# A macaron layer on one core: four row blocks turned by SBUF transfers and VectorE instead of TensorE

## The reference

```python
x = x + 0.5 * ffn(layernorm(x))
x = x + attn(layernorm(x))
x = x + 0.5 * ffn(layernorm(x))

def ffn(x):
    x_prev = concat([zeros(B, 1, C), x[:, :-1, :]], axis=1)
    xr = mu_r * x + (1 - mu_r) * x_prev
    xk = mu_k * x + (1 - mu_k) * x_prev
    r = sigmoid(xr @ W_r.T)
    return r * (square(relu(xk @ W_k.T)) @ W_v.T)

def attn(x):                       # 16 heads of 16
    q, k = relu(x @ Wq.T) / 4, relu(x @ Wk.T) / 4
    v, u = x @ Wv.T, silu(x @ Wu.T)
    out = srms_norm(q @ (k.T @ v)) * u     # per head; k.T @ v over all tokens
    return out @ Wo.T
```

## Time and profile before

| | |
|---|---|
| median of 3 runs | 312.24 us |
| the profiled execution | 310.67 us |
| its span | 308.9 us |
| PE busy | 301.8 us, 98% |
| DVE busy | 240.9 us, 78% |
| ACT busy | 235.5 us, 76% |
| POOL busy | 215.1 us, 70% |
| granted TensorE clock | 1.0 of full speed throughout |

### The profile page before, as it was taken

One profiled execution on the slowest core, in us unless ns is written; L12 is line 12 of the kernel. 1 busy time (PEld: TensorE's weight loads), 2 busy tenths in 40 slices (PEclk: granted clock), 3 DMA queues, 4 the chain that ended last, 5 costly groups with the idle time before them and its releaser, 6 DMA issues.

```text
span 308.9 us, 5806 instructions
## 1 busy us (share of the span) xinstructions
PE 301.8 (98%) x2035; PEld 275.2 (89%) x2035; DVE 240.9 (78%) x585; ACT 235.5 (76%) x461; POOL 215.1 (70%) x237
## 2 busy tenths in 40 slices
PE   6999999999999999999999999999999999999995
PEld 4888889988988998998988998989999999999984
DVE  5899875666856946985994799596989797999695
ACT  3979669699589679679269358579797979699981
POOL 4598978789687686669278315726797979758823
PEclk9999999999999999999999999999999999999999
DMA  7960000000000000000000000000001011101123
GB/s 217 382 217 3 0 1 2 2 0 0 3 0 3 0 0 2 0 2 0 0 3 1 2 0 0 2 1 3 0 3 68 11 59 36 35 2 68 39 100 136
DMA packets 10752, 10.85 MB, mean 35 GB/s; under 512 B 482, under 2 KB 10724, under 8 KB 10724
## 3 DMA queue, kind: packets, MB, share of 16 engines
q1 hardware_dynamic: 10432, 10.23, 9.6%
q10 hardware_dynamic: 292, 0.26, 0.2%
HBM read 6.29 MB, written 4.19 MB: 34 GB/s over the span
## 4 chain that ended last, share of the span: by engine, by line
PE 74%; DVE 14%; ACT 4%; POOL 3%; issue 2%; DMA 1%; DVEq 0%; ACTq 0%
PE psK L1293 7%; PE psK L1295 7%; PE psK L1294 7%; PE psX L1293 7%; PE psX L1295 7%; PE psX L1294 7%; PE psRV L1293 6%; PE psRV L1294 6%; PE psRV L1295 6%; DVE mix L957 3%; PE psA L1310 3%; PE psA L1498 2%; PE psX L1511 2%; PE psX L1425 2%; PE psK L1498 2%
## 5 line engine op out<-in xcount | busy, mean ns | idle before, releaser
L957 DVE SCALAR_TENSOR_TENSOR mix<-psA,mu,mix 128x512 f32<-128x512 f32 x60 | 41.5, 745 | 10.0 <-ACT mix L642 10.0
L625 ACT ACTIVATE xn<-xs,shiftA,rstdA 128x256 f32<-128x256 f32 x53 | 27.7, 607 | 16.3 <-POOL shiftA L417 16.3
L433 POOL TENSOR_TENSOR mix_k_lo<-mix,mix_k_hi 128x512 fp32r<-128x512 f32 x26 | 33.2, 1299 | 8.2 <-ACT mix_k_hi L675 8.2
L642 ACT ACTIVATE mix<-psA,one_mu 128x511 f32<-128x511 f32 x60 | 36.9, 697 | 0.0
L1293 PE MATMUL psRV<-ffn_hi,mix_r_hi 128*128 128x256 f32 x120 | 34.3, 286 | 0.0
L1295 PE MATMUL psRV<-ffn_hi,mix_r_lo 128*128 128x256 f32 x120 | 33.6, 280 | 0.0
L1294 PE MATMUL psRV<-ffn_lo,mix_r_hi 128*128 128x256 f32 x120 | 33.5, 279 | 0.0
L1293 PE MATMUL psRV<-ffn_hi,act_hi 128*128 128x256 f32 x96 | 27.5, 287 | 0.2 <-POOL act_lo L455 0.2
L1294 PE MATMUL psRV<-ffn_lo,act_hi 128*128 128x256 f32 x96 | 26.8, 280 | 0.0
L1295 PE MATMUL psRV<-ffn_hi,act_lo 128*128 128x256 f32 x96 | 26.8, 279 | 0.0
L485 POOL TENSOR_TENSOR k_lo<-k_tok,k_hi 128x512 fp32r<-128x512 f32 x14 | 18.1, 1292 | 11.5 <-ACT k_hi L730 11.5
(11 more groups left out here) (210 smaller groups left out, 1081.3 us busy)
## 6 DMA issues: line engine op xcount, KB each, us to landing
xs<-x_dram SPq DMA_DIRECT2D x7, 512.0 KB, 7.8
out_dram<-xs SPq DMA_DIRECT2D x7, 512.0 KB, 2.9
out_dram<-xs SPq DMA_DIRECT2D x4, 128.0 KB, 1.8
xs<-x_dram ACTq DMA_DIRECT2D x2, 128.0 KB, 2.8
xs<-x_dram SPq DMA_DIRECT2D x2, 128.0 KB, 2.6
silu_u<-w_ffn_k_dram SPq DMA_DIRECT2D x1, 256.0 KB, 4.7
silu_u<-w_ffn_r_dram SPq DMA_DIRECT2D x1, 256.0 KB, 5.8
q_store<-w_k_dram SPq DMA_DIRECT2D x1, 256.0 KB, 6.0
```

The costliest lines, as they stand in the source:

```text
L433: nc.gpsimd.tensor_tensor(mix_k_lo[:, h, :], mix[:, 0, h, :], mix_k_hi[:, h, :].bitcast(F32), ALU.subtract).then_inc(s_lo_k, 1)
L625: nc.scalar.activation(xn[:, t, :], tile_row(xs, b, t), ACT.Identity, bias=shiftA[:, t:t + 1], scale=rstdA[:, t:t + 1]).then_inc(s_xn, 1)
L642: nc.scalar.activation(mix[:, rk, h, 1:BLOCK], psA[:, h, 0:BLOCK - 1], ACT.Copy, scale=one_mu[:, rk, h:h + 1]).then_inc(s_prev, 1)
L957: nc.vector.scalar_tensor_tensor(out=m, in0=psA[:, h, :], scalar=mu[:, rk, h:h + 1], in1=m, op0=ALU.mult, op1=ALU.add).then_inc(s_mix, 1)
```

## The change

For the blocks 3, 4, 5 and 6 (`TURNED`), the eight transposes of `transpose_a` on PE go. In their place SP issues 16 transfers inside SBUF for each block, each of a 32x32 grid element of the 4x4 grid of the 128x128 squares (32 partitions, 8 pieces of 32 float32 each): they move row group i and column group j to their place in `quads`, a view of the tile `squares`. Then `turn` on DVE transposes the 32x32 squares, two instructions of 128x512, from `quads` to `psA`. The normalized rows are written to `xn` and `gout` by turns. The rows are made an iteration ahead: those of block i+2 are made in iteration i, as before, but now from scales that POOL makes first in that iteration, and from statistics that DVE makes in the iteration before (from block 5 on); the turn on DVE comes an iteration later, where PE's transposes were. Block 3 is made within iteration 1 and turned in iteration 2.

```diff
+        TURNED = range(3, 7)
+        QUAD = 32
+        QUADS = P // QUAD
+        quads = squares[:].rearrange("p g e -> p (g e)")
+        def rows_of(n):
+            return gout if n in TURNED and n % 2 == 0 else xn
+        def turned_before(n):
+            return 2 * n - 2 * (n in TURNED and n > TURNED[0])
...
+            for n in TURNED:
+                sp.wait_ge(*normalized(n, TILES - 1))
+                if n > TURNED[0]:
+                    sp.wait_ge(s_tA, 2 * n)
+                for j in range(QUADS):
+                    for i in range(QUADS):
+                        rows = quads[j * QUAD:(j + 1) * QUAD, i * D:(i + 1) * D]
+                        sp.dma_start(rows.rearrange("c (th f) -> c th f", f=QUAD),
+                                     rows_of(n)[i * QUAD:(i + 1) * QUAD, :, :].rearrange(
+                                         "c t (h j f) -> c (t h) j f", h=HALVES, j=QUADS)[:, :, j, :]
+                                     ).then_inc(s_quads, 16)
...
             for i in range(1, 6):
+                if 2 <= i <= 4:
+                    scales_a(i + 2)
                 act_low(i)
+                if i == 1:
+                    scales_a(3)
                 k_low(i + 1)
                 if i > 1:
                     kt_low(i - 1)
-                scales_a(i + 2)
+                if i == 5:
+                    scales_a(7)
                 scales_b(i)
...
-                    act.wait_ge(s_tA, 2 * n)
+                    act.wait_ge(s_tA, turned_before(n))
...
-                    nc.scalar.activation(xn[:, t, :], tile_row(xs, b, t), ACT.Identity,
+                    nc.scalar.activation(rows_of(n)[:, t, :], tile_row(xs, b, t), ACT.Identity,
...
                 if i == 1:
                     x2_high(a)
-                activate_k(i)
-                if a is not None and i > 1:
+                    activate_k(i)
+                else:
+                    if i in (3, 4):
+                        normalize(i + 2, (0, 1))
+                    activate_k(i, (0,))
                     x2_high(a)
+                    activate_k(i, (1,))
+                    if i == 2:
+                        normalize(4)
+                    elif i < 5:
+                        normalize(i + 2, (2, 3))
                 if nxt is not None:
                     previous(nxt)
...
-                if i <= 5:
+                if i in (1, 5):
                     normalize(i + 2)
...
+            def turn(n, free=()):
+                for s, v in free:
+                    dve.wait_ge(s, v)
+                dve.wait_ge(s_halo, n + 1)
+                dve.wait_ge(s_quads, 16 * QUADS * QUADS * (n - TURNED[0] + 1))
+                blocks = quads.rearrange("p (i t h f) -> p h t i f", i=QUADS, t=TILES, h=HALVES)
+                for h in range(HALVES):
+                    nc.vector.transpose(psA[:, h, :].rearrange("p (t i c) -> p t i c", t=TILES, i=QUADS),
+                                        blocks[:, h, :, :, :]).then_inc(s_tA, 1)
...
-            def projections(a):
+            def projections(a, n=None):
                 for t in range(TILES):
+                    if n is not None:
+                        bn_rows(n, (t,))
                     silu(a, t)
 
             for i in range(1, 7):
-                if 1 < i <= 5:
-                    stats_a(i + 2)
+                if i == 2:
+                    stats_a(4)
+                if 3 <= i <= 5:
+                    turn(i + 1, {4: [(s_wcen, 4)], 5: [(s_kvbd, 1)]}.get(i, ()))
                 if i > 1:
                     x2_low(i - 1)
+                if i == 2:
+                    turn(3)
                 mix_current(i + 1)
                 if i == 1:
                     stats_a(3)
-                projections(i - 1)
+                projections(i - 1, i + 3 if 2 <= i <= 4 else None)
...
                 stats_b(i)
+                if 2 <= i <= 4:
+                    bn_all(i + 3)
                 r_low(i + 1)
...
-                transpose_a(i + 1, [(s_wcen, 4)] if i == 4 else [])
                 transpose_b(i - 1)
...
-            transpose_a(6, [(s_kvbd, 1)])
```

More of the change, by code:

```diff
@@ L168, in macaron @@
         s_tA = sem("s_tA")
+        s_quads = sem("s_quads")
         s_prev = sem("s_prev")
```

## The result

The changed kernel takes 324.1 us (median of 4 runs, 321.9 to 324.5); the kernel before took 311.6 us beside it (4 runs, 310.4 to 312.5). The ratio is 1.039, with a 95% interval of 1.033 to 1.045: slower, and near the 322.5 us that were forecast. The profiled execution took 324.14 us, its span is 322.4 us.

What follows compares the result with a forecast made beforehand. PE's list bounds the kernel before; after the change a loop over ACT, DVE and POOL would. The transposes would give 3.5 us, the waits take 14.6: 310.67 + 12.0 - 0.87 = 321.8, median 322.5 us, range 317 to 331.

Steps and rivals of the forecast that it cites:

- The bound: Before, PE's work list sets the time; after, a loop over ACT, DVE and POOL longer than PE's about 21 us.
- Faster: Rival: POOL's scales are done before ACT reaches them, PE keeps the whole 3.5 us gain, 307.2 us; chance 0.05.
- The place of the wait: Iteration 3: ACT's first tiles of block 5 wait for POOL's `scales_a(5)`, so PE stands 3.7 us at `k_and_u(2)`.
- The ring: From iteration 3, ACT, DVE and POOL wait on each other in turn, 26.0 us an iteration; chance 0.76.
- The scales' time in iteration 3: POOL finishes `scales_a(5)`, behind `x1_low(2)` and `wo_lo`, at 73.25 us.
- The transfers: SP's 16 transfers a block, 0.47 us an issue: block 3 lands near 50.7 us, just in time for its turn.
- D: Time from a block's finished rows to its last transfer's landing: 11.4 us taken, 9 to 25 us as ends.
- The pieces: 4096 pieces of 128 B a block, 256 for each of 16 engines, at 45 ns each: 11.6 us.
- slow transfers: Rival: short pieces make D 25 us, block 3 lands at 64.3, total 337 us; chance 0.12.
- The turn: Two 128x512 transposes on DVE, 0.65 us each, 1.3 us together; nothing lost in iterations 3 to 5.
- The wait comes once: Rival: only iterations 2 and 3 lose, 2.0 + 3.7 us, total 313.8 us; chance 0.07.
- The sum: Whole program: 310.67 + 12.0 lost up to `kv(0)` - 0.87 gained in iteration 5 = 321.8 us.

Runs made afterwards that it cites:

- The order alone: Changed kernel with PE's transposes back for all blocks, no transfers or DVE turn, changed order of statistics, scales and rows kept: 323.0 us, ratio 1.038.
- The kernel with three blocks: Against the kernel before: blocks 4 to 6 moved and turned, block 3 on PE, rows of 5 and 6 in ACT's old gap: 309.57 us, ratio 0.9966.

## Why the prediction was right, step by step

- **The bound.** Right: PE's list set the time before, and the loop over ACT, DVE and POOL sets it after. The order alone costs as much as the change. But the wait for scales, which the forecast made the deciding term, is only about half of it: with that wait gone, the tiles in ACT's full stretch still cost 5.8 us in iterations 2 to 5, through PE's waits for `k_lo` and `g_acc`. The forecast had the tiles in its ring, as the 2 us that ACT grew by; that they cost without the wait it only mentions, without a number, under its rival "Faster".
- **The place of the wait.** Right: ACT's rows wait for POOL's `shiftA`, 5.55 us in iteration 3 and 4.29 in iteration 4; about 6 were forecast. `k_and_u(2)` waited 3.15 us, forecast 3.7.
- **The ring.** Forecast 26.0, measured 25.28 us. What I set too high was POOL's share: 7.15 us forecast, 6.4 measured. `var_epsA` and `var_epsB` take 0.19 us in these turns, and 0.52 and 0.55 in the rows I took them from the earlier trace rows, where DVE's `xs` and `mix_r_lo` run beside them.
- **The scales' time in iteration 3.** From the start of iteration 2 it is 29.8 us, forecast 29.5. Two misses nearly cancel here: `previous(3)` and with it `stats_b(2)` came about 1 us later than I said (`stats_b(2)` ends 22.0 us after the start, forecast 21.1), and from there POOL took 7.8 us, forecast 8.4. That is luck.
- **The transfers.** D was 12.7 us (41.26 to 53.93), I took 11.4. The mis-sized term is the issue: 0.70 us of SP's queue for each of block 3's transfers (0.65 to 0.67 for the later blocks) instead of the 0.47 of one weight; the weights in the same queue took 0.43 to 0.93 before, so one row was too little to price it by. That made DVE wait 2.38 us in iteration 2, but ACT, which had its tiles to do, only 0.64. By its own sign ("if DVE sits at `turn` for more than 2 us") this part of the forecast was wrong, and it had set the sign badly: what counts is what reaches ACT and PE. Iteration 2 came to 24.09, forecast 23.2.
- **The pieces.** My price for a packet was far too high. The queue's packets rose by 17,408, its time by (0.132 x 322.4 - 0.096 x 308.9) x 16 = 206 us: 12 ns each, not 45. The 256 pieces of a block on one engine need 3 us, less than the 10.4 that SP needs to issue them. So the rival of the slow transfers falls. Short pieces still cost more for a byte: 206 us for 2.10 MB is 0.10 ns a byte of an engine's time, where the packets of before took 0.046. By the Trainium skill, page "DMA: Bandwidth & Descriptors", section "Why small descriptors are slow (HBM only)", transfers inside SBUF don't suffer the penalty. The trace agrees in that nothing near the feared 91 ns a piece shows; that there is no penalty at all it doesn't show.
- **The turn.** Forecast 1.3 us for two instructions, measured 1.31. In iterations 3 to 5 it cost nothing, as forecast.
- **The wait comes once.** Fell: iterations 3 and 4 both lost, 5.3 and 3.4 us.
- **Faster.** Fell for the reason given: scales at 75.9, ACT free at 70.4. The kernel with three blocks shows that the mechanism exists, with the scales at their old place.
- **The sum.** I had +12.0 up to `kv(0)` and -0.87 in iteration 5, together +11.1. Measured from the start of iteration 2: +11.5 and -0.73, together +10.8. Inside it two misses offset each other, which is luck again: iteration 2 lost 2.9 us where I had 2.0, iterations 3 and 4 lost 8.6 where I had 10.0. The rest of the 12.5 to 13.5 us is mainly the spread of the first product, which I didn't have in the sum at all.

Open is what makes the first 16 matmuls take 3.7 us in one execution and 5.5 in the next; no run was aimed at it. The start of the kernel with three blocks still loses 0.6 us, and could perhaps be ordered better; that wasn't tried.

## What to carry to other kernels

Look not at how full an engine is but at where in its iteration the free time lies: the same four tiles of 2 us an iteration cost next to nothing in ACT's gap, and about 11 us over three iterations in its full stretch. About half of that was a late input from POOL that held up everything behind it; the other half stayed when nothing waited for that input. Before work is moved an iteration ahead, walk the ring over all engines, add it up, and compare it with the list of the engine that bounds. And a chain of small transfers is priced by its issues, so put a whole iteration between them and their reader.

## What the runs showed of the hardware

- A transfer of 32 KB in 256 pieces of 128 B takes SP's queue 0.65 to 0.70 us to issue (16 in 10.4 to 11.3); one of 128 KB in 1024 pieces took 0.7 us (4 in 2.8) to 1.0 us (4 in 3.9); a weight's 256 KB took 0.43 to 0.93.
- Operations of two operands on POOL and DVE slowed each other down where they ran at once. DVE's add of 128x512 took 0.69 us at 65.74, where POOL idled, and 1.70 us while POOL ran the operation below, which itself took 2.96 us instead of the 2.54 and 2.56 of its like in iterations 2 and 3 (first DVE's row, then POOL's, of the changed kernel):

```profile
39.23 1.70 DVE L1076 TENSOR_TENSOR xs<-xs,gate 128x512 f32<-128x512 f32 x1
```

```profile
39.10 2.96 POOL L459 TENSOR_TENSOR mix_k_lo<-mix,mix_k_hi 128x512 fp32r<-128x512 f32 x2
```

- In iteration 3, after PE had stood idle from 76.97 to 80.12 us, the granted clock of the window was 0.94 instead of 1.00, in the changed kernel and in the one with the order alone. By windows of 1 us it was 0.50, the lower of its two levels (1.2 of 2.4 GHz), from 81 to 83 us, and 1.00 again from 84 on. The matmuls of `k_and_u(2)` show it (PE, changed kernel):

```profile
80.88 0.63 PE L1352 MATMUL psX<-att_hi,x_lo 128*128 128x512 f32 x1
...
84.07 0.39 PE L1351 MATMUL psX<-att_lo,x_hi 128*128 128x512 f32 x1
```

PE's busy time went up with it, 22.89 us for 130 instructions where iteration 2 had 21.40 for 129. It cost nothing that shows: ACT works from 75.93 to 90.76 us without a wait for PE.
- The first product's matmuls took 0.38 us each (median) in the kernel before and 0.62 in the changed one, at a granted clock of 1.00 in both. That is nearly the ratio of the two rows above. Whether it has the same cause isn't shown.
